# An LSTM over 512 steps on one core: scales per row for Wx, Wx split while it arrives, and steps 1 and 2 from float32 operands

## The reference

```python
xW = einsum('ntd,dg->ntg', x, Wx) + b          # [32, 512, 2048]
def step(carry, xw_t):                          # 512 of them, one after the other
    prev_h, prev_c = carry
    a = xw_t + prev_h @ Wh
    i, f, o = sigmoid(a[:, :H]), sigmoid(a[:, H:2*H]), sigmoid(a[:, 2*H:3*H])
    g = tanh(a[:, 3*H:])
    next_c = f * prev_c + i * g
    next_h = o * tanh(next_c)
    return (next_h, next_c), next_h
out = x + hs                                    # hs: all the next_h
```

## Time and profile before

| | |
|---|---|
| median of 3 runs | 2572.32 us (2572.17 to 2572.68) |
| profiled execution, its own time | 2571.03 us |
| its span | 2569.2 us |
| TensorE busy | 2519.4 us (98%) |
| VectorE busy | 2125.0 us (83%) |
| ScalarE busy | 1535.5 us (60%) |
| GpSimd busy | 51.3 us (2%) |
| mean granted TensorE clock | 0.993 |

### The profile page before, as it was taken

The page is one execution under the profiler, slowest core; times in us unless marked ns, Lnnn a source line. Parts: engine busy times, 40 slices in busy tenths (PEclk is TensorE's granted clock), DMA queues, the critical chain, the costliest instruction groups (busy, mean ns, idle before and its releaser), DMA issues.

```text
span 2569.2 us, 166266 instructions
## 1 busy us (share of the span) xinstructions
PE 2519.4 (98%) x67392; PEld 1803.4 (70%) x67392; DVE 2125.0 (83%) x8738; ACT 1535.5 (60%) x5780; POOL 51.3 (2%) x134
## 2 busy tenths in 40 slices
PE   4999999999999999999999999999999999999998
PEld 1677777777777777777777777777777777777775
DVE  7888888888888888888888888888888888888887
ACT  5666565566656556565656656566665655666564
POOL 0000000000000000000000000000000000000000
PEclk7999999999999999999999999999999999999999
DMA  6111111111111111111111111111111111111111
GB/s 157 39 41 37 42 44 37 37 47 39 37 43 43 37 37 46 39 37 43 43 37 38 47 37 37 44 42 37 39 47 37 37 45 41 37 40 46 37 37 27
DMA packets 223581, 109.84 MB, mean 43 GB/s; under 512 B 25280, under 2 KB 222528, under 8 KB 222528
## 3 DMA queue, kind: packets, MB, share of 16 engines
q1 hardware_dynamic: 223456, 109.45, 17.0%
q10 hardware_dynamic: 96, 0.03, 0.0%
HBM read 75.83 MB, written 33.55 MB: 43 GB/s over the span
## 4 chain that ended last, share of the span: by engine, by line
PE 96%; DVE 1%; SPq 1%; DMA 1%; ACT 1%; issue 0%; ACTq 0%; DVEq 0%
PE Z L345 71%; PE run L345 19%; PE extra L345 6%; DMA wh_raw<-in_Wh 1%; SPq L262 1%; DVE wx_lo L766 0%; ACT wx_hi L552 0%; SPq L293 0%; ACT tanh_c L534 0%; DVE h_hi L834 0%; DVE wh_lo L771 0%; ACT wh_lo L562 0%; ACT wh_hi L556 0%; SPq L301 0%; ACT act L523 0%
## 5 line engine op out<-in xcount | busy, mean ns | idle before, releaser
L345 PE MATMUL Z<-wh_hi,hT_hi 128*32 128x512 f16 x8176 | 796.1, 379 | 9.6 <-DVE hT_hi L839 6.2
L345 PE MATMUL Z<-wh_lo,hT_hi 128*32 128x512 f16 x8176 | 796.1, 379 | 0.0
L523 ACT ACTIVATE act<-Z 128x128 f32<-128x128 f32 x1024 | 287.6, 281 | 591.7 <-PE Z L345 591.7
L345 PE MATMUL Z<-wh_hi,hT_lo 128*32 128x512 f16 x8176 | 529.7, 379 | 0.0
L534 ACT ACTIVATE tanh_c<-gc 128x64 f32<-128x64 f32 x1024 | 262.8, 257 | 312.6 <-DVE gc L860 248.7
L345 PE MATMUL run<-wx_hi,x_hi 128*32 128x256 f16 x6096 | 431.0, 273 | 14.3 <-DVE x_lo L671 13.8
L345 PE MATMUL Z<-wx_hi,x_hi 128*32 128x256 f16 x6096 | 430.7, 273 | 0.9 <-DVE wx_lo L766 0.5
L345 PE MATMUL run<-wx_lo,x_hi 128*32 128x256 f16 x6096 | 431.0, 273 | 0.0
L345 PE MATMUL run<-wx_hi,x_lo 128*32 128x256 f16 x6096 | 431.0, 273 | 0.0
L345 PE MATMUL Z<-wx_hi,x_lo 128*32 128x256 f16 x6096 | 430.7, 273 | 0.0
L345 PE MATMUL Z<-wx_lo,x_hi 128*32 128x256 f16 x6096 | 430.7, 273 | 0.0
(11 more groups left out here) (91 smaller groups left out, 4024.2 us busy)
## 6 DMA issues: line engine op xcount, KB each, us to landing
x_in<-in_x SPq DMA_DIRECT2D x512, 64.0 KB, 2.1
x_res<-in_x SPq DMA_DIRECT2D x512, 64.0 KB, 2.1
out_y<-y SPq DMA_DIRECT2D x508, 64.0 KB, 1.7
wx_raw<-in_Wx SPq DMA_DIRECT2D x16, 256.0 KB, 8.7
wh_raw<-in_Wh SPq DMA_DIRECT2D x16, 256.0 KB, 16.4
bias_bc<-in_bias SPq DMA_DIRECT2D x4, 64.0 KB, 2.2
out_y<-y SPq DMA_DIRECT2D x4, 48.0 KB, 1.6
h_in<-in_h SPq DMA_DIRECT2D x4, 16.0 KB, 13.0
```

The costliest lines, as they stand in the source:

```text
L345: return nc.tensor.matmul(out, lhsT, rhs, start=False, stop=last, skip_group_check=True)
L523: nc.scalar.activation(half_gates(act, a)[:, 0:2], half_gates(Z[s], a)[:, 0:2], ACT.Sigmoid, scale=scale).then_inc(gates_done, 1)
```

## The change

1. **Scales per row.** `Wx` gets a power of two for each partition and each of the two chunk pairs `cp` (chunks 0 and 2, chunks 1 and 3) instead of one for all. It comes from two chunks alone, with no all-reduce: `sum_of_wx` on ScalarE (sum of absolute values of a chunk, four of them), then `scale_of_rows` on VectorE (three small instructions). VectorE's four `largest_wx` reductions go. `scale_x` is therefore two activations, one for each `cp`, in every block, and the scales are five numbers and not four. The all-reduced scale stays for the scale of z.
2. **Wx split while it arrives.** The chunks come in the order 0, 2, 1, 3, and forms are made and cut for `cp = 0` while the other half is still loading; all forms of Wx are cut before step 0's gates. x and bias are loaded from ScalarE's queue, so Wx is first in SyncE's.
3. **Steps 1 and 2 from float32.** Their recurrent parts are `raw_recurrent_part(1)` and `(2)`: float32 h, transposed, against `wh_raw`, as in step 0. `scale_raw` stays for step 3 alone. `cut_wh_hi` and `cut_wh_lo` move behind step 0, and must be complete for step 3.
4. **The first block's order** is written out anew on three engines.

The core of the diff (`...` marks what is left out):

```diff
-            load_x(0, 0)
-            for j in range(NJ):
-                sp.dma_start(bias_bc[...], ...).then_inc(bias_loaded, 16)
-            load_weights(sp, wx_raw, wx_view, wx_loaded, TURNS)
+            load_weights(sp, wx_raw, wx_view, wx_loaded, WX_ARRIVE, TURNS)
...
+            def raw_recurrent_part(t):
+                pe.wait_ge(h_turned, t + 1)
+                for ch in range(NCH):
+                    if t == 0:
+                        pe.wait_ge(wh_loaded[ch], 16 * NJ)
+                    raw = by_tile(wh_raw[:, ch])
+                    for j in range(NJ):
+                        mm = add(Z[t][L * j:L * j + B, :], h_T[:, ch, :], raw[:, j], ch == NCH - 1)
+                mm.then_inc(z_done, 1)
...
-            block(0)
+            def first_block():                       # TensorE
+                raw_recurrent_part(1)
+                raw_recurrent_part(2)
+                first_product(2, 0)
+                second_products(2, 0)
+                third_products(2, 0).then_inc(p5_done, 1)
+                first_product(3, 1)
+                pe.wait_ge(z_scaled, 1)
+                recurrent_part(3, 3)
+                second_products(3, 1)
+                last_product(2, 0).then_inc(slot_done, 1)
...
-                nc.scalar.activation(forms[:, r, 0:8]..., x_T[...], ACT.Copy, scale=x_scale(r)).then_inc(x_scaled, 1)
+                for cp in range(2):
+                    nc.scalar.activation(forms[...][:, cp], x_T[...][:, cp], ACT.Copy, scale=x_scale(r, cp)).then_inc(x_scaled, 1)
...
+            for j in range(NJ):                      # ScalarE
+                sc.dma_start(x_in[L * j:L * j + B, 0], x_view[j, :, 0:TB, :]).then_inc(x_loaded[0], 16)
+            for j in range(NJ):
+                sc.dma_start(bias_bc[...], bias_view[j].partition_broadcast(B)).then_inc(bias_loaded, 16)
...
-            for ch in range(NCH):
-                cut_wx_hi(ch)
-                if ch == 1:
-                    sum_of_x(1, 1, 1)
-                sum_of_wh(ch)
-            cut_wx_hi(4)
-            sc.wait_ge(w_scale_done, 2)
-            cut_wh_hi(0)
-            scale_x(1, 1)
-            scale_raw(1)
-            cut_wh_hi(1)
-            cut_x_hi(2, 1, 1, 0)
-            set_run(2, 0, 1)
-            set_extra(2, 0, 1)
-            sc.wait_ge(z_done, 1)
-            gates(0, 0)
-            cut_wh_hi(2)
-            tanh_of_c(0)
-            cut_wh_hi(3)
-            scale_raw(2)
-            scale_raw(3)
...
+            sum_of_wx(0)
+            sum_of_wx(2)
+            sc.wait_ge(row_scale_done, 1)
+            cut_wx_hi(0, "B11", "B21", "T1")
+            sum_of_wx(1)
+            cut_wx_hi(0, "T2", "T3")
+            sum_of_wx(3)
+            cut_wx_hi(0, "B22", "T4")
+            sc.wait_ge(row_scale_done, 2)
+            cut_wx_hi(1, "B11", "B21")
+            sum_of_wh(0)
+            sum_of_x(1, 1, 1)
+            cut_wx_hi(1, "T1", "T2")
+            sum_of_wh(1)
+            cut_wx_hi(1, "T3", "B22")
+            sum_of_wh(2)
+            cut_wx_hi(1, "T4")
+            sum_of_wh(3)
+            sc.wait_ge(z_done, 1)
+            gates(0, 0)
+            tanh_of_c(0)
+            sc.wait_ge(w_scale_done, 2)
+            cut_wh_hi(0)
+            scale_x(1, 1)
+            def first_block():
+                sc.wait_ge(z_done, 2)
+                gates(1, 1); tanh_of_c(1)            # one call a line in the code
+                cut_wh_hi(1); cut_x_hi(2, 1, 1, 0); set_run(2, 0, 1); set_extra(2, 0, 1); cut_wh_hi(2)
+                sc.wait_ge(z_done, 3)
+                gates(2, 2); set_c11(2, 0); tanh_of_c(2)
+                cut_wh_hi(3); set_c12(2, 0); scale_raw(3); set_z_unscale(0, 0)
+                cut_x_hi(3, 1, 1, 1); set_run(3, 1, 1); set_extra(3, 1, 1)
+                take_p5(2, 0); set_c21(2, 0); set_c11(3, 1); sum_of_x(2, 0, 2)
+                sc.wait_ge(z_done, 4)
+                gates(3, 3); tanh_of_c(3)
+                scale_x(2, 0); sum_of_x(3, 1, 2); cut_x_hi(4, 2, 0, 0); set_c12(3, 1)
+                set_run(4, 0, 0); set_extra(4, 0, 0); set_z_unscale(1, 1)
...
-                for ch in range(NCH):                # VectorE
-                    largest_wx(ch)
-                    ...
+                make_t1(0); make_t3(0); scale_of_rows(0); make_t2(0)
+                cut_wx_lo(0, "B11", "B21"); make_t4(0); make_t1(1)
+                cut_wx_lo(0, "T1", "T2", "T3"); make_t3(1); scale_of_rows(1)
+                largest_weight(0); make_t2(1)
+                cut_wx_lo(0, "B22", "T4"); cut_wx_lo(1, "B11", "B21"); make_t4(1)
+                nc.vector.transpose(h_T, h0_in).then_inc(h_turned, 1)     # shortened
+                weight_scale(0); turn_x(1, 1, 1)
+                cut_wx_lo(1, "T1", "T2", "T3", "B22", "T4")
+                largest_weight(1); step(0); weight_scale(1); scale_tables()
+                scale_block(0, 0); scale_block(1, 1); set_h_scale(0, 0); cut_wh_lo(0)
...
+                if isinstance(t, int) and t < RAW:   # in step(t), after last_products; RAW = 2
+                    last_c(t)
+                    ...
+                    nc.vector.tensor_tensor(h32[:, :], act[:, 2 * C:3 * C], tanh_c[:, :], ALU.mult).then_inc(h32_done, 1)
+                    v.wait_ge(h32_done, t + 1)
+                    nc.vector.transpose(h_T[:, :, :], h32[:, :]...).then_inc(h_turned, 1)
+                    return
...
+            def first_block():                       # VectorE
+                add_x(0, 0, 0); step(1); first_forms(1, 1); last_forms(1, 1); add_x(0, 1, 0)
+                cut_wh_lo(1); cut_x_lo(2, 1, 0)
+                step(2); cut_wh_lo(2); cut_wh_lo(3); add_x(0, 2, 0)
+                cut_x_lo(3, 1, 1); add_extra(2, 0); set_h_scale(1, 1)
+                turn_x(2, 0, 2); scale_block(2, 0)
+                step(3); add_x(0, 3, 0); first_forms(2, 0); last_forms(2, 0)
+                cut_x_lo(4, 0, 0); turn_x(3, 1, 2); scale_block(3, 1)
```

More of the change, by code:

```diff
@@ L45, in lstm_residual @@
     TOP_X = 12
+    TOP_W = 13
     TOP_H = 14
@@ L257, in taken, with load_weights @@
             return (not isinstance(q, int) or q >= FIRST_PAIR) and within(q, NQ)
-        def load_weights(engine, raw, view, loaded, tiles):
-            for ch in range(NCH):
+        def load_weights(engine, raw, view, loaded, chunks, tiles):
+            for ch in chunks:
                 for j in tiles:
@@ L364, in _ @@
                 mm.then_inc(raw_done, 1)
[L365 to L371, removed]
+            def raw_recurrent_part(t):
[7 more added lines that the diff above has]
+                mm.then_inc(z_done, 1)
+            raw_recurrent_part(0)
             def product(k, q, e, b, col, chunks=(0, 1)):
                 f, odd = x_form[k]
-                if isinstance(q, int) and q == FIRST_PAIR:
-                    pe.wait_ge(wx_lo_cut, 2 * W_PLACE[k] + 2)
                 for cp in chunks:
+                    if isinstance(q, int) and q == FIRST_PAIR:
+                        pe.wait_ge(wx_lo_cut, CUT[k, cp] + 1)
                     for xp, wp in ((x_hi, wx_hi), (x_hi, wx_lo), (x_lo, wx_hi)):
@@ L428, in block @@
                     q, e = 2 * n + s // 2, s // 2
[L429 to L434, removed]
+                    if s % 2 == 0:
+                        pe.wait_ge(c12_added, nth(q))
+                    recurrent_part(t, s)
                     if s % 2 == 0:
@@ L577, in _ @@
             scale_x(1, 1)
-            scale_raw(1)
-            cut_wh_hi(1)
-            cut_x_hi(2, 1, 1, 0)
-            set_run(2, 0, 1)
-            set_extra(2, 0, 1)
-            sc.wait_ge(z_done, 1)
-            gates(0, 0)
-            cut_wh_hi(2)
-            tanh_of_c(0)
-            cut_wh_hi(3)
-            scale_raw(2)
-            scale_raw(3)
[L590 to L593, removed]
+            def first_block():
+                sc.wait_ge(z_done, 2)
+                gates(1, 1)
+                tanh_of_c(1)
+                cut_wh_hi(1)
+                cut_x_hi(2, 1, 1, 0)
+                set_run(2, 0, 1)
+                set_extra(2, 0, 1)
+                cut_wh_hi(2)
+                sc.wait_ge(z_done, 3)
+                gates(2, 2)
+                set_c11(2, 0)
+                tanh_of_c(2)
+                cut_wh_hi(3)
+                set_c12(2, 0)
+                scale_raw(3)
+                set_z_unscale(0, 0)
+                cut_x_hi(3, 1, 1, 1)
+                set_run(3, 1, 1)
+                set_extra(3, 1, 1)
+                take_p5(2, 0)
+                set_c21(2, 0)
+                set_c11(3, 1)
+                sum_of_x(2, 0, 2)
+                sc.wait_ge(z_done, 4)
+                gates(3, 3)
+                tanh_of_c(3)
+                scale_x(2, 0)
+                sum_of_x(3, 1, 2)
+                cut_x_hi(4, 2, 0, 0)
+                set_c12(3, 1)
+                set_run(4, 0, 0)
+                set_extra(4, 0, 0)
+                set_z_unscale(1, 1)
             def block(i, n, r):
+                if first(n):
```

(51 more changed lines are left out.)

199 lines of the change are left out of this document (109 added, 90 removed).

## The result

The changed kernel takes 2577.73 us (median of 16 runs, 2576.53 to 2579.34) against 2572.27 us before (16 runs): ratio 1.0023, 95% interval 1.0016 to 1.0030. The forecast of 2564.2 us and its range are wrong, and so is the sign. The profiled execution's span is 2575.9 us against 2569.2.

A forecast was written before the change was run, and what follows sets the result against it. The loop is bound by TensorE's work, so only the opening moves: gates(0) 13.5 us earlier, part given back, step 5 8.1 earlier. From 2571.03 that gives 2562.9, plus 1.3 for the median 2564.2; range 2559.5 to 2568.0.

The forecast's parts named there:

- The loads: Opening: Wx's first DMA goes 3.75 us earlier; Wh's end taken 1.2 us earlier, at 43.8; bounds 0 and 3.75.
- Is the cutting really hidden?: Before step 0: ScalarE's cuts and sums of Wx end at 42.2, 1.6 us before Wh's end, so nothing is added.
- a sign change only in the loop: Rival: split scale_x delays set_c11 in the loop; 0.2 us a block beyond cover gives 2589; chance 0.04.
- its mark: Start of step 5's recurrent part, 91.52 us before; if it starts d earlier with the same loop, time falls by d.
- The gain at gates(0): Step 0's gates start at 45.8 instead of 59.28, 13.5 us earlier, behind ScalarE's sum of Wh's last chunk.
- the chain from gates to turned h: Step 0 to step 1: c, tanh, h, transpose and hand-overs take 2.35 us from the gates' start.
- the raw part with its start at the low clock: Step 1's float32 recurrent part: 3.64 us at full clock plus 1.65 for the clock's start, 5.3 us.
- cut_wh_hi(2) in front of gates(2): Step 2: matmuls end at 59.5, but gates(2) stand behind ScalarE's cut_wh_hi(2), until 60.6.
- TensorE's idling of 3 us before first_product(3): Step 3: TensorE idle from 66.5 to 69.5 behind VectorE's queue; clock then falls, 1.6 us more, gates(3) at 74.4.
- the queues behind gates(3): Steps 4 to 5: ScalarE's and VectorE's queues make step 5 start 9.0 us after gates(3), at 83.4; 1.8 us are waits.
- the loop: Split scale_x adds 0.2 us a block on ScalarE, hidden by its 1.47 us idle before the next gates: 0.
- The rival of a clock that stays high: Clock stays high after step 2, despite TensorE's 3 us idling: step 5 starts at 81.8, time 2562.6; chance 0.2.

The follow-up runs named there:

- the first experiment: The changed kernel with x and bias again in front of Wx in SyncE's queue, nothing else undone: 2567.85 us, ratio to before 0.9983.
- the best kernel: The changed kernel with only the bias in front of Wx, block 1's residual x ahead of block 5's x, and cut_x_lo(3) ahead of cut_wh_lo(3): 2558.04 us.
- the two experiments: Block 1's residual x loaded ahead of block 5's x: alone on the changed kernel 2575.55 us; with x and bias also in front of Wx 2565.75 us.
- both repairs: The changed kernel with x and bias in front of Wx and block 1's residual x loaded ahead of block 5's x: 2565.75 us, ratio 0.9974.

## Why the prediction was wrong, point by point

Landmarks in us; "x, bias first" is the first experiment, whose loads of Wx start as before, so that 1.2 is to be added to the forecast for it.

| | forecast | forecast + 1.2 | x, bias first | changed kernel |
|---|---|---|---|---|
| bias there | not costed | | 6.9 | 23.3 |
| gates(0) | 45.8 | 47.0 | 47.14 | 58.39 |
| raw part of step 1 | 5.3 long | | 5.44 | 5.34 |
| gates(1) | 53.5 | 54.7 | 55.05 | 66.19 |
| gates(2) | 60.6 | 61.8 | 61.74 | 72.89 |
| gates(3) | 74.4 | 75.6 | 75.63 | 86.83 |
| step 5's recurrent part | 83.4 | 84.6 | 84.56 | 95.77 |

**The step that failed is "The loads".** It priced what the second queue does to Wx ("the second queue's transfers share the same engines") and took 1.2 us of gain. It put no price on what Wx's queued transfers do to x and the bias. They share the engines both ways: the bias came at 23.3 us and not near 7, and "Is the cutting really hidden?", which starts ScalarE's sums with the first chunk, fell with it. Shown by putting the loads back (9.9 us less) and by making the old kernel issue them so (7.8 us more). The rivals had a sign change only in the loop, where nothing happened. The rule of the Trainium skill that the prediction weighed ("DMA: Bandwidth & Descriptors", Rules for kernel authors), no bandwidth from a second queue, held: 234 GB/s from 10 to 20 us against 238 at 10 us before. It was applied to one side only.

**The loads' gain** was 1.2, bounds 0 and 3.75. In the changed kernel the time can be seen only at the small packets of the residual x behind Wh: 247 packets are moved from 41 to 42 us, where the kernel before has 43, and 135 from 42 to 43. So Wh ends about 1 us earlier, as forecast. With only the bias in front, TensorE's work on the last chunk of Wh starts at 42.52 in the best kernel, against 45.06: 2.5. In three kernels with the loads in the order of before it starts at 45.26, 46.22 and 44.88 us, so no more than "1 to 3" can be said.

**A second term was missing: SyncE's queue.** turn_x(3) was moved behind step 3, the load of x of block 5 waits for it, and the residual x stands behind that load. 2.2 and 2.1 us by the two experiments. The forecast took the start of step 5 as its mark and the time after it as unchanged; this wait lies behind the mark, between step 5 and step 6. In the profiled execution step 5 is 12.4 us later than forecast and step 6 loses 2.1 more, 14.5 of the 14.8 us by which it missed the forecast's 2562.9. The forecast listed ScalarE's and VectorE's queues for step 4 and not the one whose wait is on what they finish.

**What held.** The gain at gates(0), once the bias is in time (12.1 us in the first experiment, 13.3 with the 1.2 of the loads, against 13.5); the chain from gates to turned h (55.05 to 57.45 is 2.40, forecast 2.35); the raw part with its start at the low clock; cut_wh_hi(2) in front of gates(2), where the clock was up in step 2; TensorE's idling of 3 us before first_product(3) (2.83) with x_lo as its releaser, and the low clock after it; the queues behind gates(3); the loop. The forecast plus 1.2 for the loads and 2.1 for the residual is 2567.5 us; 2567.85 was measured for the first experiment, in whose profiled execution the clock fell before first_product(3) as forecast. One sum is off by a little: 97.64 - 94.17 is 3.47 and not 3.45, which moves nothing.

**The rival of a clock that stays high was right in part.** Whether the clock falls in those 2.8 us varies: of the seven profiled kernels with this idling it fell in five and stayed up in two. With x and bias first it fell (gates(3) 4.95 us after first_product(3) began), with the residual repaired too it did not, though the idling was the same 2.83 us:

```profile
73.08 0.29 PE L371 MATMUL run<-wx_hi,x_hi 128*32 128x256 f16 x4 [2.83 <-DVE x_lo L747]
...
76.56 0.28 ACT L564 ACTIVATE act<-Z 128x128 f32<-128x128 f32 x1 [1.60 <-PE Z L371]
```

There gates(3) came 3.48 us after. The fall costs 1.5 us where it happens (forecast 1.6). The raw part of step 2 took 3.64 us in the changed kernel and in four others, and 5.1 to 5.3 in four more, so there too the clock is sometimes low. The runs of these kernels spread more than those of the kernel before (2565.78 to 2569.54 in the ten of the first experiment, against 2570.86 to 2572.82 in sixteen), which fits that; it was not taken apart.

**Left open.** What the parts 1 (scales per row) and 2 (Wx split while it arrives) of the change are worth apart from part 3 (float32 operands) was not tried.

## What to carry to other kernels

Moving a load to another queue moves it beside the one that it used to be in front of: ask not only what starts earlier, but when the moved load now lands and what stands behind it. Here a small load with small packets, beside megabytes of queued large ones, took a median of 14.5 us to land and not 2.2; keep what everything waits for in front, in one queue. And when an instruction is moved later, look at the DMA queue whose next issue waits for it, and at what is queued behind that issue.

## What the runs showed of the hardware

- Eight DMAs of 64 KB issued from ScalarE's queue in the first 4.6 us, with 4 MB queued by SyncE: the first four landed at about 9 to 10 us, the last four at 23.2 to 23.9, in four kernels and in either order of the two tensors. With four of them in that queue x was turned at 6.8. Without the weights beside them all eight were there at 6.3 us. Over 8.5 to 23.5 us the engines moved 234 GB/s at a busy share of 1.06, so they were full the whole time.
- From 10 to 20 us the two queues moved the same number of packets (393 and 390 in the changed kernel) and 2.16 against 0.18 MB.
- TensorE's clock after 2.8 us of idling, with the same work behind it, was at its lower level in five kernels and at the upper in two (in the changed kernel granted 0.50 from 81.8 to 83.0 us; with both repairs 1.00 from 73 to 77); the price was 1.5 us.
